# Cross-attention kernel: the running sum of the probabilities built by accumulating transfers in three chains

## The chip, the cores and the metric

The kernel runs on one core of one Trainium2 chip, in a single launch. The metric is the device time in microseconds; lower is better. One core has TensorE (matrix products into the accumulation memory PSUM), VectorE, ScalarE and GpSimd (element-wise work), SyncE (here it issues the loads and stores) and 16 DMA engines that all queues share. In the rows below they are PE (PEld for its weight loads), DVE, ACT, POOL and SP.

## What is computed

One transformer layer on 8 batches of 56 tokens of width 128. Cross-attention with 16 heads of 64 over 1500 context vectors per batch, then a feed-forward block of width 512 with one expert per batch; both on a layer-normalised input and added back.

```python
kv = context @ Wkv;  k, v = jnp.split(kv, 2, axis=-1);  q = x @ Wq
dots = jnp.einsum('bhnd,bhmd->bhnm', q, k) * SCALE
dots = dots - (1.0 - mask)[:, None, :, None] * 1e6
attn = jax.nn.softmax(dots, axis=-1)
out  = jnp.einsum('bhnm,bhmd->bhnd', attn, v)          # then @ Wout + bout
# layer: x = x + attention(layernorm(x), ctx);  x = x + ffn(layernorm(x))
```

The softmax needs, for each of the 56 x 16 = 896 pairs of token and head, the sum of 1500 exponentials. This sum is what the change is about.

## The kernel before

**Folding.** Wq and Wk are multiplied at the start to `w_qk`, Wv and Wout to `w_vo`, so that scores and values are taken against the context itself. `qk` holds the folded queries of all batches, 896 columns per batch. Scores are computed in three products of rounded parts: `ctxt_hi` and `qk_hi` (rounded, cast by VectorE) and `ctxt_lo`, `qk_lo` (what the rounding left, subtracted by GpSimd).

**Tiles.** The 1500 context vectors of a batch are 12 tiles (`TM`) of 125 rows (`MT`). For tile t TensorE writes the scores into PSUM (`scores`, L373), ScalarE takes the exponential into slot t % 6 of the ring `ex` (`exponentials`, L597) and fills PSUM with the shift of tile t + 2 (`seed`, L607), and two tiles later TensorE multiplies the exponentials with the context (`probs_ctx`, L412). VectorE adds tile t - 1 to `ex_sum` at step t (`add_tile`, L755): 11 additions of 125x896 per batch, the last at step 0 of the next batch. At step 3 of the next batch TensorE multiplies `ex_sum` by a matrix of ones (`sum_jobs`, L435), which adds up the 125 rows, ScalarE takes the inverse through a logarithm and an exponential (`inverse_sums`, L620), and VectorE refines it (`drain_sum`, `refine_inverse`).

**Order.** Each engine has an order written out by hand: an `iteration` over t = 0 to 11 per batch, with the places of all smaller work in lists such as `MAX_AT` and `SUM_AT` (L121 to L141). TensorE's smaller products go through `job` (L333), which uses two PSUM banks in turn and waits until VectorE has emptied the one before the last. 21 of them per batch give the maxima of the next batch's scores (`max_job`, L428, emptied by `max_part`, L764). Batches are taken in pairs; in every second iteration the feed-forward block of a pair runs too. Batches 0 and 7 stand outside the loop.

**GpSimd** clears an identity matrix, subtracts the low parts of batch 0, and then, at t = 2, 3, 6 and 7, those of the next batch (`iteration`, L1016). Nothing in it waits for the pace of the tiles. **SyncE** loads a batch's transposed context (`load_ctxt`, L270) once the low parts of the batch before are subtracted, and the plain context (`load_ctx`, L276) once the products of the batch two before are done.

**Who may write over an exponential.** ScalarE writes tile t into its slot after TensorE's product with tile t - 6 and VectorE's addition of it:

```python
wait(act, pv_done, b.at(TM, t - RING + 1))
wait(act, ex_summed, b.at(TM - 1, max(t - RING, 1)) if t >= RING else b.at(TM - 1, t - RING + 1))
```

**At the start** the raw Wq and Wk lie in the memory of `ex`. **At the end**, for batch 7, VectorE adds the last tile, TensorE does the sum job, and the inverse, the output projection and the feed-forward block of the last half pair follow one after another.

Of the kernel before, what the change touches and what calls it, by code (L numbers as in the profile page):

```python
# [32 lines left out]
ALU = mybir.AluOpType  # L33
# [10 lines left out]
P = 128  # L44
# [56 lines left out]
def xattn_ffn(nc, x_pairs, ctx, ctx_t, mask_q, wq_t, wk_t, wv_t, w_out, b_out, w1, b1_t, w2, b2, out):  # L101
# [15 lines left out]
    RING = 6  # L117
    assert D == P and MT * TM == M and QT * P == Q and MC * KM == M and E == B and TM % RING == 0

# [29 lines left out]
    with ExitStack() as stack:  # L149
# [15 lines left out]

        ex = sb("ex", [P, RING, Q])
        ex_sum = sb("ex_sum", [P, 2, Q])
# [9 lines left out]
        wqk_raw = ex[:, :, :].rearrange("p r q -> p (r q)")[:, 0:2 * HP * P].rearrange("p (w j d) -> p w j d", w=2, j=HP)  # L177
# [26 lines left out]
        hid = sb("hid", [P, 2 * FT, TOK])  # L204
        hid_u = sb("hid_u", [P, 2 * FT, TOK])
        hid_e = sb("hid_e", [P, 2 * FT, TOK])
# [34 lines left out]

        block = stack.enter_context(nc.Block())

# [86 lines left out]
        def _(pe):  # L330
# [81 lines left out]
            def probs_ctx(b, t, between=None):  # L412

                u = b.parity
                pe.wait_ge(ex_ready, b.at(TM, t + 1))
                if t == 0:
                    pe.wait_ge(ctx_in[b.parity], b.at_every_other(16, 16))
                    wait(pe, att_ready, b.at(1, 0))
                    if b.i is None and b.off == 0:
                        pe.wait_ge(later_drained, HEADS)  # L420
                for c in range(2):
                    if c == 1 and between is not None:
                        between()
                    mm = nc.tensor.matmul(ps_a[:, c, 0:CH], ctx_sb[0:MT, u, t, :], ex[0:MT, t % RING, c * CH:(c + 1) * CH],  # L424
                                          start=(t == 0), stop=(t == TM - 1))
                mm.then_inc(pv_done, 1)
# [8 lines left out]
            def sum_jobs(b):  # L435

                pe.wait_ge(ex_summed, b.at(TM - 1, TM - 1))
                for c in range(2):
                    nc.tensor.matmul(job()[:, 0:CH], ones[0:MT, :], ex_sum[0:MT, b.parity, c * CH:(c + 1) * CH],  # L439
                                     start=True, stop=True).then_inc(job_ready, 1)  # L440
# [152 lines left out]
        def _(act):  # L593
# [3 lines left out]
            def exponentials(b, t):  # L597

                slot = t % RING
                src = ps_s[0:MT, t % 2, :, 0:CH]  # L600
                act.wait_ge(scores_ready, b.at(TM, t + 1))

                wait(act, pv_done, b.at(TM, t - RING + 1))
                wait(act, ex_summed, b.at(TM - 1, max(t - RING, 1)) if t >= RING else b.at(TM - 1, t - RING + 1))
                nc.scalar.activation(half(ex[0:MT, slot, :]), src, ACT.Exp, scale=SCALE).then_inc(ex_ready, 1)  # L605
# [132 lines left out]
        def _(dve):  # L738
# [16 lines left out]
            def add_tile(b, t):  # L755

                dve.wait_ge(ex_ready, b.at(TM, t + 1))
                dst = ex_sum[0:MT, b.parity, :]
                left = ex[0:MT, 0, :] if t == 1 else dst
                if t > 1:  # L760
                    dve.wait_ge(ex_summed, b.at(TM - 1, t - 1))
                nc.vector.tensor_tensor(dst, left, ex[0:MT, t % RING, :], ALU.add).then_inc(ex_summed, 1)  # L762
# [114 lines left out]
            def iteration(b, prepare=True, pair=None):  # L877
# [40 lines left out]
                for t in range(TM):  # L918
                    drain((t, 0))
                    between((t, 0))  # L920
                    if t > 1:
                        add_tile(b, t - 1)
                    elif t == 0 and b.off > 0:
                        add_tile(b.later(-1), TM - 1)
# [59 lines left out]
            add_tile(last, TM - 1)  # L984
# [15 lines left out]
        def _(pool):  # L1000
# [14 lines left out]

            def iteration(b, prepare=True):  # L1016
                for t in range(TM):
                    if b.off == 0 and t == FOLD_AT[-1][0] + 2:
# [5 lines left out]
                    if prepare and t in CTXT_LO_AT:  # L1024
# [5 lines left out]
                                    pattern=[[-1, P]], channel_multiplier=1).then_inc(ident_ready, 1)  # L1030
            for k in range(KM):
# [68 lines left out]
```

## Time and profile before

| | us |
|---|---|
| median of 3 runs | 408.41 (407.51 to 409.65) |
| profiled execution, its own time | 407.78 |
| its span | 406.0 |
| TensorE busy | 394.8 (97%) |
| TensorE, loading weights (beside its products) | 285.1 (70%) |
| VectorE busy | 302.7 (75%) |
| ScalarE busy | 206.1 (51%) |
| GpSimd busy | 57.6 (14%) |
| share of the 16 DMA engines | 15.5%, 19.45 MB |

The granted clock of TensorE is at full speed in all 40 slices. The span runs from the first to the last instruction; the execution's own time is 1.78 us longer. A busy time is a mean over the span and says nothing by itself of who waits for whom.

### The profile page before, as it was taken

To read this page: it belongs to the slowest core of one execution; us is meant where nothing else is said; L and a number is where in the kernel's file an instruction comes from. 1 tells how busy PE (TensorE), PEld (TensorE's weight loads), DVE (VectorE), ACT (ScalarE), POOL (GpSimd) and SP (SyncE) were. 2 spreads that over 40 slices of the span, in tenths; PEclk is the share of its full clock that TensorE was granted. 3 is DMA by queue.
4 is the path that set the end of the run, shared out by engine and by line. 5 is a ranking of instruction groups with operands and counts; after the bars stand their busy time and mean duration, and the time that the engine had idled before them with its cause. 6 is when DMAs were issued, how large, how long until landed. Compare 5 with 4: busy or idle time off the path is not lost.

```text
span 406.0 us, 5555 instructions
## 1 busy us (share of the span) xinstructions
PE 394.8 (97%) x1721; PEld 285.1 (70%) x1721; DVE 302.7 (75%) x490; ACT 206.1 (51%) x274; POOL 57.6 (14%) x47
## 2 busy tenths in 40 slices
PE   8998999999999999999999999999999999999995
PEld 7765777766776876767676877667776776676684
DVE  4889578878797689877887689877887687365443
ACT  3546354466437445565556444665366444755431
POOL 0603040600060000600060001500060000000000
PEclk9999999999999999999999999999999999999999
DMA  7660020050005000043005000161011001200000
GB/s 252 206 200 19 2 76 1 2 147 5 2 0 141 12 2 2 13 127 120 0 7 144 0 0 0 35 173 53 0 30 45 0 0 39 70 2 0 3 2 3
DMA packets 20661, 19.62 MB, mean 48 GB/s; under 512 B 904, under 2 KB 17576, under 8 KB 20648
## 3 DMA queue, kind: packets, MB, share of 16 engines
q1 hardware_dynamic: 20648, 19.45, 15.5%
q8 instruction: 8, 0.13, 0.1%
q14 instruction: 5, 0.04, 0.0%
HBM read 19.21 MB, written 0.23 MB: 48 GB/s over the span
## 4 chain that ended last, share of the span: by engine, by line
PE 93%; DVE 4%; ACT 2%; issue 1%; ACTq 0%
PE ps_a L424 35%; PE ps_s L396 28%; PE ps_x L432 10%; PE ps_x L451 4%; PE ps_x L439 3%; PE ps_a L371 2%; PE ps_s L526 2%; PE ps_x L471 2%; PE ps_x L480 2%; PE ps_s L410 2%; PE ps_x L344 1%; PE ps_s L364 1%; DVE log_sum L793 1%; PE ps_a L344 1%; ACT inv_sum L635 1%
## 5 line engine op out<-in xcount | busy, mean ns | idle before, releaser
L424 PE MATMUL ps_a<-ex,ctx_sb 125*128 125x448 f32 x384 | 172.2, 541 | 0.0
L605 ACT ACTIVATE ex<-ps_s 125x896 f32<-125x896 f32 x96 | 88.0, 917 | 118.9 <-PE ps_s L396 92.8
L765 DVE TENSOR_REDUCE chunk_max<-ps_x 128x1 f32<-128x500 f32 x168 | 111.2, 673 | 31.9 <-PE ps_x L432 28.9
L432 PE MATMUL ps_x<-ctxt_hi,qk_hi 128*128 128x500 f32 x168 | 88.6, 530 | 4.9 <-DVE log_sum L793 3.6
L424 PEld LDWEIGHTS ps_a<-ex,ctx_sb 125*128 125x128 f32 x384 | 71.3, 189 | 27.6 <-issue 21.6
L762 DVE TENSOR_TENSOR ex_sum<-ex_sum,ex 125x896 f32<-125x896 f32 x80 | 86.5, 1081 | 4.6 <-ACT ex L605 4.6
L396 PE MATMUL ps_s<-qk_hi,ctxt_hi 128*125 128x448 f32 x192 | 87.1, 535 | 0.0
L612 ACT COPY ps_s<-shift_row 125x896 f32<-125x896 f32 x80 | 72.9, 911 | 9.9 <-DVE shift_row L882 7.8
L396 PEld LDWEIGHTS ps_s<-qk_hi,ctxt_hi 128*125 128x125 f32 x192 | 35.8, 187 | 35.5 <-issue 35.1
L396 PE MATMUL ps_s<-qk_hi,ctxt_lo 128*125 128x448 f32 x192 | 57.2, 379 | 0.0
L396 PE MATMUL ps_s<-qk_lo,ctxt_hi 128*125 128x448 f32 x192 | 54.7, 366 | 0.0
L1007 POOL TENSOR_TENSOR qk_lo<-qk,qk_hi 128x448 fp32r<-128x448 f32 x16 | 23.7, 1483 | 217.5 <-DVE qk_hi L786 216.0
L432 PEld LDWEIGHTS ps_x<-ctxt_hi,qk_hi 128*128 128x128 f32 x168 | 31.5, 188 | 24.8 <-issue 8.1
L396 PEld LDWEIGHTS ps_s<-qk_hi,ctxt_lo 128*125 128x125 f32 x192 | 35.6, 186 | 6.8 <-issue 2.6
L396 PEld LDWEIGHTS ps_s<-qk_lo,ctxt_hi 128*125 128x125 f32 x192 | 35.6, 185 | 3.3
L1013 POOL TENSOR_TENSOR ctxt_lo<-ctxt_raw,ctxt_hi 128x500 fp32r<-128x500 f32 x24 | 32.0, 1348 | 11.3 <-DVE ctxt_hi L782 11.3
L782 DVE CAST ctxt_hi<-ctxt_raw 128x500 fp32r<-128x500 f32 x24 | 23.7, 1019 | 0.0
L793 DVE TENSOR_TENSOR log_sum<-ps_x,inv_sum 128x448 f32<-128x448 f32 x16 | 9.3, 619 | 18.6 <-ACT inv_sum L635 18.6
L451 PEld LDWEIGHTS ps_x<-w_vo,att_n 128*128 128x128 f32 (+1 forms) x160 | 18.1, 170 | 1.5 <-issue 1.2
L451 PE MATMUL ps_x<-w_vo,att_n 128*128 128x128 f32 (+1 forms) x160 | 18.6, 275 | 0.0
L629 ACT ACTIVATE log_sum<-ps_x 128x448 f32<-128x448 f32 x16 | 8.7, 542 | 10.7 <-PE ps_x L439 10.6
L648 ACT ACTIVATE logv<-veps 128x1 f32<-128x1 f32 (+2 forms) x7 | 1.4, 203 | 24.7 <-DVE veps L828 22.5
(79 smaller groups left out, 272.4 us busy)
## 6 DMA issues: line engine op xcount, KB each, us to landing
ctxt_raw<-in_ctx_t SPq DMA_DIRECT2D x8, 750.0 KB, 7.3
ctx_sb<-in_ctx SPq DMA_DIRECT2D x8, 750.0 KB
w_sb<-in_w SPq DMA_DIRECT2D x4, 512.0 KB, 3.7
w_sb<-in_w SPq DMA_DIRECT2D x8, 256.0 KB, 4.3
ex<-in_wq_t SPq DMA_DIRECT2D x2, 256.0 KB, 3.8
ex<-in_wk_t SPq DMA_DIRECT2D x2, 256.0 KB, 4.6
att_n<-in_wv_t SPq DMA_DIRECT2D x1, 512.0 KB, 6.0
att_n<-in_w_out SPq DMA_DIRECT2D x1, 512.0 KB, 6.8
```

The costliest lines, as they stand in the source:

```text
L396: mm = nc.tensor.matmul(dst[c], a[:, u, rows], q[:, u, chunks[c]], start=(n == 0 and not seed), stop=(n == 2 and seed), skip_group_check=seed)
L424: mm = nc.tensor.matmul(ps_a[:, c, 0:CH], ctx_sb[0:MT, u, t, :], ex[0:MT, t % RING, c * CH:(c + 1) * CH], start=(t == 0), stop=(t == TM - 1))
L432: nc.tensor.matmul(bank[:, 0:MC], qk_hi[:, u, t * P:(t + 1) * P], ctxt_hi[:, u, k * MC:(k + 1) * MC], start=True, stop=True).then_inc(job_ ...
L451: mm = nc.tensor.matmul(bank[pair.tokens(), 0:D], att_n[:, h, pair.tokens()], w_vo[:, h, :], start=(h == 0), stop=(h == HEADS - 1))
L605: nc.scalar.activation(half(ex[0:MT, slot, :]), src, ACT.Exp, scale=SCALE).then_inc(ex_ready, 1)
L612: nc.scalar.copy(ps_s[0:MT, t % 2, :, 0:CH], half(shift_row[0:MT, :])).then_inc(seeded, 1)
L762: nc.vector.tensor_tensor(dst, left, ex[0:MT, t % RING, :], ALU.add).then_inc(ex_summed, 1)
L765: nc.vector.tensor_reduce(chunk_max[:, k, t:t + 1], filled()[:, 0:MC], AX.X, ALU.max).then_inc(job_free, 1)
L782: nc.vector.tensor_copy(ctxt_hi[:, b.parity, k * MC:(k + 1) * MC], ctxt_raw[:, k * MC:(k + 1) * MC]).then_inc(ctxt_hi_ready, 1)
L793: nc.vector.tensor_tensor(log_sum[:, cols], bank[:, 0:CH], inv_sum[:, cols], ALU.mult).then_inc(job_free, 1)
L1007: nc.gpsimd.tensor_tensor(qk_lo[:, b.parity, cols], b.pick(qk)[:, cols], qk_hi[:, b.parity, cols].bitcast(F32), ALU.subtract).then_inc(qk_ ...
L1013: nc.gpsimd.tensor_tensor(ctxt_lo[:, b.parity, cols], ctxt_raw[:, cols], ctxt_hi[:, b.parity, cols].bitcast(F32), ALU.subtract).then_inc(c ...
```

## The change

Tiles 0, 1 and 2 of a batch are no longer written into the ring but into three accumulators, `ex_first`, which exist twice, for even and odd batches. The ring `ex_ring` has four slots and holds tiles 3 to 11 in turn. GpSimd issues one DMA for each of tiles 3 to 10 that adds the tile, 128 partitions by 896 numbers, to accumulator t % 3 (`add_by_dma`). The three chains are 0, 3, 6, 9; 1, 4, 7, 10; and 2, 5, 8. A transfer waits for the one before it in its chain. VectorE makes three additions per batch (`add_to_sum`), at steps 0, 1 and 2 of the next batch: tile 11 to the third accumulator, then the first and the second accumulator to it. ScalarE's exponential waits for the transfer that reads its slot instead of VectorE's addition. GpSimd clears the part of the accumulators that doesn't hold the raw Wq and Wk, and the ring, at the start, because the transfers take all 128 partitions and the exponentials write 125. The raw weights lie in `ex_first`. The tiles of the feed-forward block (`hid`, `hid_u`, `hid_e`) lie in the memory of `w_qk`, which is no longer read by then.

```diff
@@ -114,8 +114,8 @@
     TOK = 64
-    RING = 6
-    assert D == P and MT * TM == M and QT * P == Q and MC * KM == M and E == B and TM % RING == 0
+    RING, ACCS, LAST_DMA = 4, 3, 10
+    assert D == P and MT * TM == M and QT * P == Q and MC * KM == M and E == B and ACCS < RING < LAST_DMA < TM
@@ -163,8 +163,8 @@
-        ex = sb("ex", [P, RING, Q])
-        ex_sum = sb("ex_sum", [P, 2, Q])
+        ex_first = sb("ex_first", [P, 2, ACCS, Q])
+        ex_ring = sb("ex_ring", [P, RING, Q])
         shift_diag = sb("shift_diag", [P, QT, P], F32R)
@@ -174,7 +174,7 @@
-        wqk_raw = ex[:, :, :].rearrange("p r q -> p (r q)")[:, 0:2 * HP * P].rearrange("p (w j d) -> p w j d", w=2, j=HP)
+        wqk_raw = ex_first[:, :, :, :].rearrange("p u r q -> p (u r q)")[:, 0:2 * HP * P].rearrange("p (w j d) -> p w j d", w=2, j=HP)
         wvo_raw = att_n[:, :, :].rearrange("p (w j) d -> p w j d", w=2)
@@ -201,9 +201,7 @@
         z_t = sb("z_t", [P, P])
-        hid = sb("hid", [P, 2 * FT, TOK])
-        hid_u = sb("hid_u", [P, 2 * FT, TOK])
-        hid_e = sb("hid_e", [P, 2 * FT, TOK])
+        hid, hid_u, hid_e = (w_qk[:, 4 * k:4 * k + 4, :].rearrange("p (g c) (h n) -> p (g c h) n", g=1, n=TOK) for k in range(3))
         out_sb = sb("out_sb", [P, D])
@@ -239,7 +237,20 @@
+        add_may_go = sem("add_may_go")
+        ex_added = [sem("ex_added_first"), sem("ex_added_second"), sem("ex_added_third")]
+        ADDS = [sum(t % ACCS == j for t in range(ACCS, LAST_DMA + 1)) for j in range(ACCS)]
+        DVE_SUMS = TM - 1 - LAST_DMA + ACCS - 1
+
         block = stack.enter_context(nc.Block())
+
+        def ex(b, t):
+
+            return ex_first[:, b.parity, t, :] if t < ACCS else ex_ring[:, (t - ACCS) % RING, :]
+
+        def dma_added(eng, b, t):
+
+            eng.wait_ge(ex_added[t % ACCS], b.at(16 * ADDS[t % ACCS], 16 * (t // ACCS)))
@@ -421,7 +432,7 @@
                         between()
-                    mm = nc.tensor.matmul(ps_a[:, c, 0:CH], ctx_sb[0:MT, u, t, :], ex[0:MT, t % RING, c * CH:(c + 1) * CH],
+                    mm = nc.tensor.matmul(ps_a[:, c, 0:CH], ctx_sb[0:MT, u, t, :], ex(b, t)[0:MT, c * CH:(c + 1) * CH],
                                           start=(t == 0), stop=(t == TM - 1))
@@ -434,9 +445,9 @@
-                pe.wait_ge(ex_summed, b.at(TM - 1, TM - 1))
+                pe.wait_ge(ex_summed, b.at(DVE_SUMS, DVE_SUMS))
                 for c in range(2):
-                    nc.tensor.matmul(job()[:, 0:CH], ones[0:MT, :], ex_sum[0:MT, b.parity, c * CH:(c + 1) * CH],
+                    nc.tensor.matmul(job()[:, 0:CH], ones[0:MT, :], ex_first[0:MT, b.parity, ACCS - 1, c * CH:(c + 1) * CH],
                                      start=True, stop=True).then_inc(job_ready, 1)
@@ -596,13 +607,21 @@
-                slot = t % RING
                 src = ps_s[0:MT, t % 2, :, 0:CH]
...
-                wait(act, pv_done, b.at(TM, t - RING + 1))
-                wait(act, ex_summed, b.at(TM - 1, max(t - RING, 1)) if t >= RING else b.at(TM - 1, t - RING + 1))
-                nc.scalar.activation(half(ex[0:MT, slot, :]), src, ACT.Exp, scale=SCALE).then_inc(ex_ready, 1)
+                if t >= ACCS + RING:
+                    act.wait_ge(pv_done, b.at(TM, t - RING + 1))
+                    dma_added(act, b, t - RING)
+                elif t >= ACCS and (b.i is not None or b.off > 0):
+                    act.wait_ge(pv_done, b.at(TM, 0))
+                    before = b.later(-1)
+                    last = max(s for s in range(ACCS, TM) if (s - t) % RING == 0)
+                    if last <= LAST_DMA:
+                        dma_added(act, before, last)
+                    else:
+                        act.wait_ge(ex_summed, before.at(DVE_SUMS, last - LAST_DMA))
+                nc.scalar.activation(half(ex(b, t)[0:MT, :]), src, ACT.Exp, scale=SCALE).then_inc(ex_ready, 1)
@@ -752,14 +771,21 @@
-            def add_tile(b, t):
-
-                dve.wait_ge(ex_ready, b.at(TM, t + 1))
-                dst = ex_sum[0:MT, b.parity, :]
-                left = ex[0:MT, 0, :] if t == 1 else dst
-                if t > 1:
-                    dve.wait_ge(ex_summed, b.at(TM - 1, t - 1))
-                nc.vector.tensor_tensor(dst, left, ex[0:MT, t % RING, :], ALU.add).then_inc(ex_summed, 1)
+            def add_to_sum(b, n):
+
+                dst = ex_first[0:MT, b.parity, ACCS - 1, :]
+                if n < TM - 1 - LAST_DMA:
+                    t = LAST_DMA + 1 + n
+                    dve.wait_ge(ex_ready, b.at(TM, t + 1))
+                    dve.wait_ge(pv_done, b.at(TM, ACCS))
+                    dma_added(dve, b, max(s for s in range(LAST_DMA + 1) if s % ACCS == ACCS - 1))
+                    part = ex(b, t)[0:MT, :]
+                else:
+                    j = n - (TM - 1 - LAST_DMA)
+                    dma_added(dve, b, max(s for s in range(LAST_DMA + 1) if s % ACCS == j))
+                    part = ex_first[0:MT, b.parity, j, :]
+                wait(dve, ex_summed, b.at(DVE_SUMS, n))
+                nc.vector.tensor_tensor(dst, dst, part, ALU.add).then_inc(ex_summed, 1)
@@ -918,10 +944,8 @@
                     between((t, 0))
-                    if t > 1:
-                        add_tile(b, t - 1)
-                    elif t == 0 and b.off > 0:
-                        add_tile(b.later(-1), TM - 1)
+                    if t < DVE_SUMS and b.off > 0:
+                        add_to_sum(b.later(-1), t)
                     between((t, 1))
@@ -981,7 +1005,8 @@
             iteration(last, prepare=False, pair=Pair(None, ROUNDS, half=0))
-            add_tile(last, TM - 1)
+            for n in range(DVE_SUMS):
+                add_to_sum(last, n)
             for c in range(2):
@@ -1013,8 +1038,20 @@
+            def add_by_dma(b, t):
+
+                pool.wait_ge(ex_ready, b.at(TM, t + 1))
+                if t < 2 * ACCS:
+                    pool.wait_ge(pv_done, b.at(TM, t % ACCS + 1))
+                else:
+                    dma_added(pool, b, t - ACCS)
+                pool.sem_inc(add_may_go, 1)
+                pool.dma_start(ex_first[:, b.parity, t % ACCS, :], ex(b, t), accum_op=ALU.add).then_inc(ex_added[t % ACCS], 16)
+
             def iteration(b, prepare=True):
                 for t in range(TM):
+                    if ACCS < t <= LAST_DMA + 1:
+                        add_by_dma(b, t - 1)
                     if b.off == 0 and t == FOLD_AT[-1][0] + 2:
@@ -1028,6 +1065,8 @@
                                     pattern=[[-1, P]], channel_multiplier=1).then_inc(ident_ready, 1)
+            nc.gpsimd.memset(ex_first[:, :, :, :].rearrange("p u r q -> p (u r q)")[:, 2 * HP * P:], 0.0)
+            nc.gpsimd.memset(ex_ring[:, :, :], 0.0)
             for k in range(KM):
```

## Rows read from the trace of the kernel before

**Rows 1.** The page's busy times: engine, busy us (share of span), instructions.

```profile
PE 394.8 (97%) x1721; PEld 285.1 (70%) x1721; DVE 302.7 (75%) x490; ACT 206.1 (51%) x274; POOL 57.6 (14%) x47
```

**Rows 2.** Chain that ended last, in order of time: start us, us, what.

```profile
84.46 1.52 PE ps_x L439 x4
...
125.55 1.52 PE ps_x L439 x4
...
173.86 1.52 PE ps_x L439 x4
```

**Rows 3.** Waits of TensorE: who for whom, us in total, times, longest.

```profile
PE ps_x L432 <- DVE log_sum L793: 3.6, 6, 0.6
...
PE ps_x L432 <- DVE chunk_max L765: 1.0, 1, 1.0
```

**Rows 4.** Page, costliest groups: out<-in forms xcount, busy us, mean ns, idle before.

```profile
L762 DVE TENSOR_TENSOR ex_sum<-ex_sum,ex 125x896 f32<-125x896 f32 x80 | 86.5, 1081 | 4.6 <-ACT ex L605 4.6
```

**Rows 5.** Timeline, batch 2's iteration: start us, us, engine, line, what.

```profile
119.81 1.48 DVE L765 TENSOR_REDUCE chunk_max<-ps_x 128x1 f32<-128x500 f32 x2
...
121.98 0.38 PE L432 MATMUL ps_x<-ctxt_hi,qk_hi 128*128 128x500 f32 x1
```

**Rows 6.** Timeline, exponentials of tiles 3, 7 and 10 of batch 1.

```profile
87.38 0.91 ACT L605 ACTIVATE ex<-ps_s 125x896 f32<-125x896 f32 x1
...
100.00 0.92 ACT L605 ACTIVATE ex<-ps_s 125x896 f32<-125x896 f32 x1 [1.25 <-PE ps_s L396]
...
109.62 0.92 ACT L605 ACTIVATE ex<-ps_s 125x896 f32<-125x896 f32 x1 [1.32 <-PE ps_s L396]
```

**Rows 7.** Timeline, VectorE, batch 2's iteration: first cast, addition at t = 2.

```profile
115.62 1.36 DVE L782 CAST ctxt_hi<-ctxt_raw 128x500 fp32r<-128x500 f32 x1
...
123.00 1.08 DVE L762 TENSOR_TENSOR ex_sum<-ex 125x896 f32<-125x896 f32 x1
```

**Rows 8.** DMA issues: queue, count, KB each, median us to landing.

```profile
ctxt_raw<-in_ctx_t SPq DMA_DIRECT2D x8, 750.0 KB, 7.3
...
w_sb<-in_w SPq DMA_DIRECT2D x4, 512.0 KB, 3.7
...
x_tok<-in_x SPq DMA_DIRECT2D x1, 256.0 KB, 2.7
```

**Rows 9.** Timeline of SyncE: time that issuing a DMA took.

```profile
1.22 0.42 SPq L268 DMA_DIRECT2D ex<-in_wq_t  x1
...
81.19 5.03 SPq L274 DMA_DIRECT2D ctxt_raw<-in_ctx_t  x1
```

**Rows 10.** Groups of GpSimd: its subtraction and its clearing of 2048 elements.

```profile
L1013 POOL TENSOR_TENSOR ctxt_lo<-ctxt_raw,ctxt_hi 128x500 fp32r<-128x500 f32 x24 | 32.0, 1348 | 11.3 <-DVE ctxt_hi L782 11.3
...
L1021 POOL MEMSET att_n<- 128x2048 f32 x1 | 1.8, 1805 | 13.9 <-DVE chunk_max L765 13.9
```

**Rows 11.** Windows, a stretch of loads: busy by engine, clock, DMA share, GB/s.

```profile
181.00:190.00 9.00, 9.00 (x36) 6.56 (x35) 7.17 (x11) 5.12 (x6) 0.00 (x0) 1.00 0.57 196
```

**Rows 12.** Timeline of the start: GpSimd's instructions, VectorE's normalisation and copy.

```profile
1.19 0.29 POOL L1029 TENSOR_SCALAR_AFFINE_SELECT ident<-ident 128x128 f32<-128x128 f32 x1 [0.24 <-POOL ident L1027]
...
5.96 0.34 DVE L945 TENSOR_SCALAR log_sum<-x_tok,meanvar,rstd 128x128 f32<-128x128 f32 x1
...
7.84 0.29 DVE L874 COPY inv_sum<-ps_x 128x128 f32<-128x128 f32 x1 [1.53 <-PE ps_x L519]
...
10.60 4.09 POOL L1013 TENSOR_TENSOR ctxt_lo<-ctxt_raw,ctxt_hi 128x500 fp32r<-128x500 f32 x3 [9.12 <-DVE ctxt_hi L782]
```

**Rows 13.** Timeline, VectorE, the same cast with GpSimd quiet.

```profile
32.02 0.41 DVE L782 CAST ctxt_hi<-ctxt_raw 128x500 fp32r<-128x500 f32 x1
```

**Rows 14.** Timeline of the end: exponential of tile 10, last addition, sum job.

```profile
377.75 0.92 ACT L605 ACTIVATE ex<-ps_s 125x896 f32<-125x896 f32 x1 [0.52 <-PE ps_s L396]
...
382.45 1.07 DVE L762 TENSOR_TENSOR ex_sum<-ex_sum,ex 125x896 f32<-125x896 f32 x1
...
386.00 1.67 PE L439 MATMUL ps_x<-ex_sum,ones 125*128 125x448 f32 x4
```

## The prediction, made before the changed kernel had run

> **What bounds the kernel now.** I read the busy times first: TensorE works 394.8 us of a span of 406.0 us, VectorE 302.7, ScalarE 206.1, GpSimd 57.6 [rows 1]. The reader should see that the engine which the change unloads is not the one that is full. The chain that ended last, in order of time, gives the pace: its sum jobs stand at 84.46, 125.55 and 173.86, so an iteration lasts 41.1 us, or 48.3 where a pair's output runs too [rows 2]. Then the waits of TensorE: inside the loop it waits for VectorE six times, 3.6 us in all, for the multiplication that empties the column sums, and once for a maximum, 1.0 us [rows 3]. The 3.6 us stay whatever VectorE's load, because that multiplication itself waits for ScalarE's exponential of the logarithm. So the body runs at the pace of TensorE's columns, and an edit gains there only by taking columns off TensorE. This one takes none.
>
> **What leaves VectorE.** Eleven additions of 125x896 per batch, 88 in all, at 1081 ns [rows 4] become three per batch, 24 in all. 88 x 1.08 = 95.1 us falls to 25.9 us, so VectorE's busy time falls by 69 us, to about 234. Of that, TensorE sees at most the 1.0 us wait for a maximum: the other work of VectorE fits already. I take 0 (bounds: a gain of 1.0 us, or 4.6 us if the 3.6 us went too).
>
> **The step at t = 1.** Before, VectorE had no addition at t = 1; now it joins the first chain there, 1.08 us between the last cast and the first two maxima. In batch 2 those two run from 119.81 to 121.29, and TensorE's third maximum job, which needs the first one's bank, starts at 121.98 [rows 5]. Moved back by 1.08, the first maximum (half of 1.48 us) ends at about 121.6 and the second at 122.3, in front of the jobs that need their banks (the fourth, 0.63 us after the third, about 122.6). Slack 0.3 us, cost 0; if it misses, up to 1.08 us in each of seven iterations, 7.6 us. At t = 0 an addition stood before, and so did one at t = 2.
>
> **The eight transfers per batch.** Nothing in this trace accumulates by DMA or is issued from GpSimd, so three costs are unknown: GpSimd's issue, the time to landing, and how much of the 16 DMA engines one takes. What covers them is read from the times of the exponentials. In batch 1 tile 3's ends at 87.38 + 0.91 = 88.3, tile 7's starts at 100.0, tile 10's ends at 109.62 + 0.92 = 110.5 [rows 6]; that is 3.2 us per tile. Three deadlines follow. (a) Exponential t writes over tile t-4 of the ring of four, so each transfer of tiles 3 to 7 has 100.0 - 88.3 = 11.7 us to land. Behind that wait stand ScalarE's seed and the next scores, so a miss reaches TensorE within a tile. (b) VectorE needs the last transfer, tile 10's, at t = 2 of the next iteration, where the addition started at 123.00 [rows 7]: 12.5 us after its exponential. Behind that addition stands the sum job of TensorE, at 125.55 in the chain [rows 2], 2.5 us later. (c) All eight must be served between 88.3 and 123.0: 34.7 us.
>
> Time to landing: plain loads took 2.7 us for 256 KB, 3.7 for 512 KB and 7.3 for 750 KB [rows 8]. One transfer here is 128 x 896 x 4 bytes = 448 KB. Interpolated, a plain one lands in 3.45 us. An accumulating one must also read its destination; I add the slope once more, 448 x 1.0/256 = 1.75, which gives 5.2 us. Lower bound 3.45, upper bound twice the 7.3 us row by its bytes, 2 x 7.3 x 448/750 = 8.7 us. GpSimd's issue: a DMA issue on the other queue took 0.42 us, and 5.03 us where that queue was full [rows 9]; GpSimd's own subtraction takes 1.35 [rows 10]. I take 1.3. Together 6.5 us (3.9 to 13.7), inside (a) and (b) at the value taken. GpSimd pays 64 x 1.3 = 83 us and was idle for 348.
>
> Share of the DMA engines: at 181 to 190 us loads moved 196 GB/s with the engines 57% busy, 344 GB/s when full [rows 11]. By that a plain 448 KB takes 1.3 us of all engines, a doubled one 2.7. The load of the next transposed context takes 2.2 us more of the same window at that rate. Eight times 2.7 + 2.2 + 2 for the last landing = 26 us against 34.7. The limit is (34.7 - 4.2)/8 = 3.8 us each. I take 2.7, cost 0; both ends are 1.3 and 8.7. A collective's reduce step is put down to its second source read and not to the adder in the Trainium skill, Collectives: The Full Stack, section The bandwidth ceiling; doubling once more is that rule, and no row here can show it.
>
> **What moves on GpSimd and SyncE.** The three subtractions for the next batch's low halves stood at t = 2, 6 and 7 only in program order: GpSimd ran ahead of them. Now transfers stand between, each waiting for its exponential, so the last subtraction comes behind tile 6's transfer, whose exponential starts 3.2 us before tile 7's and ends at 97.7 [rows 6]. Add 1.3 and 1.35: 100.4. SyncE issues the next load of the transposed context after it, where it did so at 81.19 [rows 9]. VectorE's first cast needs it at 115.62 [rows 7]: 15 us for a transfer of 7.3. Cost 0; at twice the time, 14.6 us, still 0. TensorE needs the low halves only at the next t = 0. ScalarE's exponential has one more wait, which costs nothing while (a) holds.
>
> **The start.** GpSimd clears 6912 elements per partition. It cleared 2048 in 1.8 us [rows 10], so 6.1 us, from 1.5 (its last instruction, 1.19 + 0.29) to 7.6, before its first subtraction at 10.60 [rows 12]. Hidden by 3 us, cost 0. If VectorE's copies can't run beside it, the normalisation due at 5.96 ends at 7.9 instead of 6.3, and the copy at 7.84, which needs a transposition between them, starts some 0.5 us late [rows 12]. That such a thing exists is seen in the cast of 128x500: 0.41 us with GpSimd quiet, 1.36 us beside its subtraction [rows 13]. Bounds 0 and 1.1 us (two such blocks), value 0. The Trainium skill, SBUF — State Buffer, Who interferes with whom, says that VectorE's two-port copies and GpSimd lock each other out for a whole instruction; by it the start would be 0.5 us later and the sum 0.5 us higher. The cast rows agree for subtractions; no row shows a clear beside a copy.
>
> **The end.** This is the one place without cover. Before, the last addition ran at 382.45 and was done at 383.5, while TensorE's products went on until the sum job at 386.00 [rows 14]. Now three additions stand there in a row: tile 11 at 382.45 to 383.5, first chain to 384.6, second chain (tile 10 in it) to 385.7 if its transfer has landed by 384.6. Tile 10's exponential ends at 377.75 + 0.92 = 378.7 [rows 14]; plus 6.5 it lands at 385.2. The last addition is then done at 386.3, the hand-over takes 0.15, and the sum job starts at 386.45: 0.5 us later. Nothing runs beside it from there. Lower end 0 (landing by 384.6), upper end with 13.7: landing 392.4, sum job 393.6, 7.6 us. With the upper landing alone (8.7 + 1.3): 388.7, sum job 389.9, 3.9 us.
>
> **Sum.** The profiled execution took 407.78 us, 1.78 more than its span. 407.78 + 0 (body) + 0 (start) + 0.5 (end) = 408.3. The median of the runs before lies 0.63 above the profiled execution, so the forecast is 408.9 us.
>
> **Rivals.**
> 1. The body is hidden, but a transfer lands later than I take: 10 to 13.7 us after its exponential. For it: every row of a transfer is of another kind and another queue. Against: 512 KB in 3.7 us. End 3.9 to 7.6 us later, body at the edge of deadline (a). Time: 408.4 + 3.9 = 412.3, up to 416.
> 2. The other side: the DMA engines (or GpSimd's issue) can't serve one accumulation per tile. It decides above 3.8 us each. At 4.36 (the 7.3 us row by bytes, once) the eight need 8 x 4.36 + 4.2 = 39.1 us against 34.7: 4.4 us per batch. The long iterations have 7 us more room than the short ones [rows 2]. Four short ones give 18 us: 426. At 5.03 (the blocked issue) 8 x 5.03 + 4.2 - 34.7 = 9.7, in the short ones 39 us and 3 x 2.7 = 8 in the long: 455. At 8.7 the transfers alone are 64 x 8.7 = 557 us: above 600. For it: an addition in the path of a DMA is nowhere in this trace. Against: the rate rows leave 1.1 us per transfer even with the second read.
> 3. VectorE's relief gives back what TensorE waits for it in the body: 4.6 us, 408.4 - 4.6 = 403.8. Against: 3.6 of them wait for ScalarE.
> That the transfers aren't made, or that VectorE keeps its additions, I exclude by the diff.
>
> **How the numbers follow.** Forecast (hidden body, end 0 to 1.6 us, start 0 to 1.1 us; own range 407.6 to 410.4) 0.60. Rival 1: 0.12. Rival 2: 0.22. Rival 3: 0.06. About 0.5%, 2.0 us, is what a measurement of this kernel can tell from no change. Faster by more is rival 3: 0.06. Same is the forecast and the near edge of rival 1: 0.62. Slower is the rest: 0.32. The range runs from 407.0 (below the forecast's lower edge; rival 3 left out, 0.06) to 428, which takes in rival 1 and the mild case of rival 2 and leaves out about 0.14.
>
> **What would show it.** VectorE's busy time near 234 us with 24 additions of 125x896. TensorE's waits in the body still the 3.6 us after the sums and no wait of ScalarE for a transfer. Landing times near 5 us and a share of the DMA engines up from 15% by some 64 x 2.7/406 = 43 points. In the last batch, the third addition ending near 386.3 and the sum job right behind it. I am wrong if TensorE's busy share falls in the short iterations with ScalarE or VectorE waiting for a DMA ahead of it (rival 2), if the gap at the end is over 2 us (rival 1), or if iterations get shorter than 41 us (rival 3).

## The result, and the profile after

The changed kernel takes 414.4 us (median of 4 runs, 413.8 to 417.6) against 408.3 before: 1.017 times as long (1.014 to 1.019). That is inside the range I gave, and on the side that I gave 0.32. The likeliest case, no change, did not happen. The profiled execution took 414.44 us with a span of 412.6, 6.6 more than before.

The page of the changed kernel: busy times, the new DMA queue, the issues on GpSimd, and the time to landing. They answer to [rows 1, 8].

```profile
PE 397.5 (96%) x1721; PEld 286.5 (69%) x1721; DVE 255.1 (62%) x426; ACT 206.1 (50%) x274; POOL 117.8 (29%) x113
...
q0 software_dynamic: 9216, 29.36, 38.4%
...
L1049 POOL DMA_DIRECT2D ex_first<-ex_ring x64 | 55.9, 873 | 224.7 <-ACT ex_ring L624 221.2
...
ex_first<-ex_ring POOLq DMA_DIRECT2D x64, 448.0 KB, 4.4
```

VectorE fell from 302.7 to 255.1 us, not to 234. Some 13 us of the 21 are instructions that became longer: without the two collisions found below (experiment 3) VectorE is busy 241.8 us. Where the other 8 are was not tested; a record of an addition overlaps the next one's by up to 0.1 us (133.05 + 1.08 against 134.05 in experiment 9), so that leaving 64 out frees less than 64 x 1.08. TensorE, whose work is the same, rose by 2.7: some of it ran at a lower clock. The 64 transfers took 0.87 us each to issue, 4.4 us to land and 38.4% of the DMA engines, 2.5 us each.

Where the 6.6 us are is seen by comparing the starts of the 96 exponentials in the two traces. The lag is 4.67 us at the very first and stays there within 0.2 us through batches 0 and 1. It grows by some 0.6 us in each of batches 2, 4 and 6, most of it between tiles 7 and 9 (taken at tile 2 of batches 1, 3, 5 and 7 it is 4.67, 5.30, 5.95 and 6.55), and is 6.56 at the last one and at the last sum job. So there are two places, and the end is not one of them.

**The start.** Timeline of the changed kernel (start us, us, engine, line, what); the last row is the first exponential:

```profile
1.43 2.87 POOL L1068 MEMSET ex_first<- 128x3328 f32 x1
...
1.52 5.88 DVE L977 TENSOR_SCALAR ident<-ident 128x128 f32<-128x128 f32 x1 [0.25 <-POOL ident L1066]
...
4.24 3.09 POOL L1069 MEMSET ex_ring<- 128x3584 f32 x1
...
9.63 0.34 DVE L969 TENSOR_SCALAR log_sum<-x_tok,meanvar,rstd 128x128 f32<-128x128 f32 x1
...
10.60 0.29 DVE L900 COPY inv_sum<-ps_x 128x128 f32<-128x128 f32 x1 [0.63 <-PE ps_x L530]
...
10.94 3.76 PE L375 MATMUL ps_s<-inv_sum,w_qk 128*128 128x112 f32 x16 [0.38 <-DVE inv_sum L900]
...
37.01 0.92 ACT L624 ACTIVATE ex_first<-ps_s 125x896 f32<-125x896 f32 x1 [0.45 <-PE ps_s L421]
```

VectorE's first multiplication, 0.23 us of work, took 5.88 us: it ended 0.07 us after GpSimd's second clear did. The normalisation that stood at 5.96 us [rows 12] came at 9.63 and the copy at 10.60 instead of 7.84. The same two rows of before, the query products and the first exponential:

```profile
8.31 2.01 PE L364 MATMUL ps_s<-inv_sum,w_qk 128*128 128x112 f32 x16 [0.51 <-ACT w_qk L689]
...
32.34 0.92 ACT L605 ACTIVATE ex<-ps_s 125x896 f32<-125x896 f32 x1 [0.46 <-PE ps_s L410]
```

The query products begin 2.6 us later and then take 3.76 us instead of 2.01. Windows from 10 to 14 and from 14 to 16 us (length, busy us and instructions of PE, PEld, DVE, ACT and POOL, granted clock, DMA share, GB/s) of the changed kernel, then the first of them for the kernel before:

```profile
10.00:14.00 4.00, 3.50 (x15) 3.24 (x16) 2.70 (x11) 0.78 (x2) 1.14 (x1) 0.50 0.76 288
...
14.00:16.00 2.00, 2.00 (x12) 1.67 (x12) 0.62 (x2) 0.78 (x2) 2.00 (x3) 0.62 0.36 109
```

```profile
10.00:14.00 4.00, 4.00 (x25) 2.86 (x24) 3.17 (x8) 2.19 (x5) 3.40 (x3) 1.00 0.75 290
```

TensorE had idled, and ran this stretch at half of full speed, 1.2 instead of 2.4 GHz: the granted clock fell at 8.7 us, during a wait from 8.1 to 10.1, and was back at 15.5. The two add up: 2.63 of delay and 1.75 in the query products are 4.4 of the 4.67.

**The pair iterations.** Sum jobs in the chain, to be read beside [rows 2]: the short iteration still takes 41.1 us, the long one 48.9 instead of 48.3.

```profile
89.13 1.52 PE ps_x L450 x4
...
130.21 1.52 PE ps_x L450 x4
...
179.16 1.52 PE ps_x L450 x4
```

Timeline of the changed kernel at tile 6 of batch 2, and the same normalisation before:

```profile
147.69 0.87 POOL L1049 DMA_DIRECT2D ex_first<-ex_ring  x1 [4.54 <-ACT ex_ring L624]
...
147.70 2.25 DVE L859 TENSOR_SCALAR z<-x,meanvar,rstd 128x128 f32<-128x128 f32 x1
...
148.29 1.56 POOL L1038 TENSOR_TENSOR ctxt_lo<-ctxt_raw,ctxt_hi 128x500 fp32r<-128x500 f32 x1
...
150.66 0.33 PE L472 MATMUL ps_x<-ident,z 128*128 128x128 f32 x1 [0.42 <-DVE chunk_max L791]
```

```profile
144.02 0.34 DVE L833 TENSOR_SCALAR z<-x,meanvar,rstd 128x128 f32<-128x128 f32 x1
```

The normalisation `z` took 2.25 us instead of 0.34. It ended with GpSimd's subtraction, which used to run at step 1 and now stands behind tile 6's transfer. VectorE's maxima come late behind it, and TensorE waits for a bank before it can transpose `z`.

TensorE's waits, to be read beside [rows 3]. The second and the last are the start (there TensorE waits for the normalised input and, before that, for raw weights), the third the three pair iterations, with 1.2 of the 1.9 us that these lose; the other two are as before.

```profile
PE ps_x L443 <- DVE log_sum L819: 3.6, 6, 0.6
...
PE ps_x L530 <- DVE log_sum L969: 2.0, 1, 2.0
...
PE ps_x L472 <- DVE chunk_max L791: 1.2, 3, 0.4
...
PE ps_x L443 <- DVE chunk_max L791: 1.0, 1, 1.0
...
PE ps_a L355 <- DMA ex_first<-in_wk_t: 0.8, 1, 0.8
```

**The end.** To be read beside [rows 14]: exponential of tile 10, its transfer's issue, the three additions, the sum job.

```profile
384.31 0.92 ACT L624 ACTIVATE ex_ring<-ps_s 125x896 f32<-125x896 f32 x1 [0.52 <-PE ps_s L407]
...
385.83 0.86 POOL L1049 DMA_DIRECT2D ex_first<-ex_ring  x1 [1.86 <-ACT ex_ring L624]
...
389.01 1.07 DVE L788 TENSOR_TENSOR ex_first<-ex_first,ex_ring 125x896 f32<-125x896 f32 x1
...
390.19 2.29 DVE L788 TENSOR_TENSOR ex_first<-ex_first 125x896 f32<-125x896 f32 x2
...
392.56 1.74 PE L450 MATMUL ps_x<-ex_first,ones 125*128 125x448 f32 x4
```

Products and additions finish together: the sum job is as far behind the exponential as before, 8.25 us in both.

### The profile page after: what moved, and what is told of

Read it like the earlier page. It is cut to its first block, busy times and chain, and to the rows that moved or that the text cites. A ratio compares the mean times of both kernels' runs of the same rounds, so it can differ in the third digit from the quotient of the medians.

```text
span 412.6 us, 5552 instructions
## 1 busy us (share of the span) xinstructions
PE 397.5 (96%) x1721; PEld 286.5 (69%) x1721; DVE 255.1 (62%) x426; ACT 206.1 (50%) x274; POOL 117.8 (29%) x113
## 3 DMA queue, kind: packets, MB, share of 16 engines
q0 software_dynamic: 9216, 29.36, 38.4%
## 4 chain that ended last, share of the span: by engine, by line
PE 88%; DVE 7%; issue 3%; ACT 1%; POOL 0%; DVEq 0%; ACTq 0%; POOLq 0%
PE ps_a L435 33%; PE ps_s L407 26%; PE ps_x L443 10%; PE ps_x L462 4%; PE ps_x L450 3%; PE ps_a L382 2%; PE ps_x L482 2%; PE ps_x L491 2%; PE ps_s L421 2%; DVE ident L977 1%; PE ps_s L375 1%; PE ps_x L355 1%; DVE chunk_max L791 1%; DVE log_sum L819 1%; ACT inv_sum L654 1%
## 5 line engine op out<-in xcount | busy, mean ns | idle before, releaser
L435 PE MATMUL ps_a<-ex_ring,ctx_sb 125*128 125x448 f32 x288 | 128.8, 541 | 0.0
L1049 POOL DMA_DIRECT2D ex_first<-ex_ring x64 | 55.9, 873 | 224.7 <-ACT ex_ring L624 221.2
L624 ACT ACTIVATE ex_ring<-ps_s 125x896 f32<-125x896 f32 x72 | 66.0, 917 | 92.8 <-PE ps_s L407 91.5
L435 PEld LDWEIGHTS ps_a<-ex_ring,ctx_sb 125*128 125x128 f32 x288 | 53.4, 190 | 21.2 <-issue 17.0
L435 PE MATMUL ps_a<-ex_first,ctx_sb 125*128 125x448 f32 x96 | 43.6, 540 | 0.0
L1038 POOL TENSOR_TENSOR ctxt_lo<-ctxt_raw,ctxt_hi 128x500 fp32r<-128x500 f32 x24 | 35.1, 1465 | 8.7 <-DVE ctxt_hi L808 8.7
L624 ACT ACTIVATE ex_first<-ps_s 125x896 f32<-125x896 f32 x24 | 22.1, 919 | 29.1 <-PE ps_s L421 27.8
L808 DVE CAST ctxt_hi<-ctxt_raw 128x500 fp32r<-128x500 f32 x24 | 22.8, 980 | 0.0
L435 PEld LDWEIGHTS ps_a<-ex_first,ctx_sb 125*128 125x128 f32 x96 | 18.0, 189 | 5.7 <-issue 4.0
```

The source lines that it names most:

```text
L624: nc.scalar.activation(half(ex(b, t)[0:MT, :]), src, ACT.Exp, scale=SCALE).then_inc(ex_ready, 1)
L808: nc.vector.tensor_copy(ctxt_hi[:, b.parity, k * MC:(k + 1) * MC], ctxt_raw[:, k * MC:(k + 1) * MC]).then_inc(ctxt_hi_ready, 1)
L1038: nc.gpsimd.tensor_tensor(ctxt_lo[:, b.parity, cols], ctxt_raw[:, cols], ctxt_hi[:, b.parity, cols].bitcast(F32), ALU.subtract).then_inc(c ...
L1049: pool.dma_start(ex_first[:, b.parity, t % ACCS, :], ex(b, t), accum_op=ALU.add).then_inc(ex_added[t % ACCS], 16)
```

## The experiments

Each ran beside the kernel before on the same chip, whose medians were 408.0 to 408.2. The first exponential's start varies by up to 1 us between profiled executions that do the same there (31.95 to 32.90 in the five versions with the clears moved behind), so smaller differences between two profiles are not read there; inside one profile the lag is steadier.

### 1. The clears moved behind (e1)

```diff
-memset(ex_first rest); memset(ex_ring)      # ahead of batch 0's subtractions
+qk_lo_chunk(0, 0); memset(ex_first rest); memset(ex_ring); qk_lo_chunk(0, 1)
```

> The changed kernel with GpSimd's two clears moved from the front to between its two subtractions of the first queries' low half (about 17 to 23 us), where VectorE does only maxima and additions. Theory A (VectorE's constant multiplication at 1.5 us is locked out by the clears, 5.88 us instead of 0.23, and TensorE's first work slips 2.6 us and then runs at half clock, 4.67 us in all): that multiplication back to 0.23 us, no stretch at half clock, first exponential near 32.3 instead of 37.0, time 414.3 - 4.7 = 409.7. Rival S (the start is late because the raw weights now land elsewhere and TensorE waits 0.8 us for them): no change, 414.3.

Measured 410.3, ratio 1.0054 (1.0034 to 1.0073). The first exponential starts at 32.9. Its timeline, VectorE's first multiplication and the `z` of batch 2:

```profile
1.52 0.23 DVE L977 TENSOR_SCALAR ident<-ident 128x128 f32<-128x128 f32 x1 [0.24 <-POOL ident L1066]
...
143.64 2.25 DVE L859 TENSOR_SCALAR z<-x,meanvar,rstd 128x128 f32<-128x128 f32 x1
```

4.1 of the 6.1 us are gone and the first operation is short again; `z` is as long as in the changed kernel. Rival S is out: the raw weights lie where the changed kernel has them. A wait for them can come even so without harm: in e12, which has these clears too, it is 0.9 us, and the first exponential starts at 32.34, as in the kernel before.

### 2. The subtractions moved ahead (e2)

```diff
-CTXT_LO_AT, QK_LO_AT = [2, 6, 7], [2, 3]
+CTXT_LO_AT, QK_LO_AT = [1, 2, 3], [2, 3]
```

> The changed kernel with the three subtractions of the context's low parts at t = 1, 2, 3 of GpSimd's order instead of 2, 6, 7, so that they run ahead of the transfers as they did before. Theory B (in the pair iterations the normalisation at t = 6 takes 2.25 us instead of 0.34 because GpSimd's second subtraction runs beside it, 0.63 us each, 1.9 us in three): normalisation at most 1.2 us (the issue of the transfer, 0.87 us, may still lock it), the three steps of 0.63 us gone, time 414.3 - 1.9 = 412.4. Rival T (it is the issue of the transfer alone that locks VectorE): normalisation still near 1.2 us, and part of the 1.9 stays: 413.3. Rival U (traffic of the transfers slows VectorE): normalisation stays at 2.2, time 414.3.

Measured 411.9, 2.5 less than the changed kernel. Timeline, `z` of batch 2 and the transfer's issue beside it:

```profile
150.28 0.86 POOL L1049 DMA_DIRECT2D ex_first<-ex_ring  x1 [5.81 <-ACT ex_ring L624]
...
150.30 0.35 DVE L859 TENSOR_SCALAR z<-x,meanvar,rstd 128x128 f32<-128x128 f32 x1
```

With the issue beside it and the subtraction away, `z` takes 0.35 us, and no wait for a maximum before the transposition is left. So it is the subtraction (theory B), not the issue (rival T) and not the traffic (rival U). The edit gave 0.6 us more than B said; experiment 3 shows that 0.9 us come from the iteration of batch 0.

### 3. Both (e3)

```diff
+qk_lo_chunk(0, 0); memset(ex_first rest); memset(ex_ring); qk_lo_chunk(0, 1)
+CTXT_LO_AT, QK_LO_AT = [1, 2, 3], [2, 3]
```

> Both edits: clears behind, subtractions ahead. Theories A and B together: 414.3 - 4.7 - 1.9 = 407.7, that is the kernel before within 0.5 us, since nothing else of the change is on the path. If the transfers or the two joining additions cost anything of their own, it is what remains above 408.3.

Measured 407.2, ratio 0.9975 (0.9961 to 0.9989): a little faster than before. 0.9 us of it lie in the iteration of batch 0. Timelines there, first of this version, then of the kernel before: GpSimd's first subtraction beside the casts, the casts, and TensorE's maximum job with its wait.

```profile
32.31 1.26 POOL L1038 TENSOR_TENSOR ctxt_lo<-ctxt_raw,ctxt_hi 128x500 fp32r<-128x500 f32 x1 [9.80 <-DVE ctxt_hi L808]
...
33.41 1.74 DVE L808 CAST ctxt_hi<-ctxt_raw 128x500 fp32r<-128x500 f32 x2
...
35.78 0.49 PE L443 MATMUL ps_x<-ctxt_hi,qk_hi 128*128 128x500 f32 x1 [0.15 <-DVE chunk_max L791]
```

```profile
33.41 1.25 POOL L1013 TENSOR_TENSOR ctxt_lo<-ctxt_raw,ctxt_hi 128x500 fp32r<-128x500 f32 x1
...
33.61 2.62 DVE L782 CAST ctxt_hi<-ctxt_raw 128x500 fp32r<-128x500 f32 x2
...
36.87 0.50 PE L432 MATMUL ps_x<-ctxt_hi,qk_hi 128*128 128x500 f32 x1 [1.03 <-DVE chunk_max L765]
```

With another order on GpSimd the two casts take 1.74 us instead of 2.62, and the wait of 1.03 us [rows 3] shrinks to 0.15. The same drop of the lag, 0.9 us at tile 2 of batch 0, stands in the traces of e2 and e9.

### 4. The kernel before with the clears alone (e4)

```diff
+nc.gpsimd.memset(ex rest, 3328 columns); nc.gpsimd.memset(spare, 3584 columns)   # at the front
```

> The kernel before with nothing added but the two clears by GpSimd at its front (3328 elements of the ring, 3584 of a spare tile); no transfers, additions as before. Theory A: VectorE's multiplication takes about 5.9 us, first exponential near 37.0, time 408.3 + 4.7 = 413.0. Rival S, or any that needs the transfers: 408.3.

Measured 412.3, ratio 1.0112 (1.0074 to 1.0151); single runs up to 416.1. VectorE's first multiplication, and the window from 14 to 20 us:

```profile
1.51 5.88 DVE L954 TENSOR_SCALAR ident<-ident 128x128 f32<-128x128 f32 x1 [0.24 <-POOL ident L1030]
```

```profile
14.00:20.00 6.00, 6.00 (x25) 4.79 (x23) 2.30 (x3) 1.36 (x3) 4.03 (x4) 0.50 0.64 162
```

The half clock's end, window from 22 to 24 us:

```profile
22.00:24.00 2.00, 2.00 (x13) 1.92 (x12) 0.72 (x2) 0.78 (x2) 0.00 (x0) 0.63 1.01 355
```

No transfer is needed for the loss at the start. The median is 4.1 us above the kernel before. In the profiled execution (415.9 us) the granted clock fell at 9.8 us and was back only at 23.4, with TensorE busy all the time from 11 us on, and the first exponential came 8.0 us late; in experiment 2's profile it is 8.1. In the changed kernel's profile the half clock lasted 6.8 us. So behind the same clears the half clock lasts 7 us in some executions and 14 in others. What decides is not shown: TensorE's waits differ too (2.4 and 2.3 us in the two long cases; 0.8 for the raw weights and then 2.0 in the short one). Experiment 4's six runs fall into two groups, 411.9 to 412.7 and 415.9 to 416.1, with a mean granted clock of 0.992 to 0.996 and 0.982. The changed kernel's run of 417.6 us, at 0.983 against 0.990 to 0.994, looks like the long case; it has no trace.

### 5. The wait filled with idle products (e5)

An idle product is one whose result nobody uses.

```diff
 pe.wait_ge(ident_ready, 1)
+keep_clock(12)
 xnt_job(0, 1, 1)
```

> The changed kernel as it is (clears at the front), with twelve idle products of 128 columns on TensorE ahead of the first transposition, where it waits 2.0 us for the normalised input. Theory A splits the 4.67 us of the start into 2.6 us of waiting and some 2 us of half clock behind it (the 16 query products take 3.76 us instead of 2.01). With the wait filled, the granted clock stays at full speed in the stretch from 10 to 14 us and the time falls by about 2 us: 412.3. Rival K (the half clock doesn't come from the wait, or the clock was low anyway): the stretch stays at 0.5 and the time at 414.3.

Measured 412.8 (412.3 to 414.6), 1.6 less than the changed kernel. Window from 10 to 14 us:

```profile
10.00:14.00 4.00, 3.62 (x30) 3.24 (x29) 3.46 (x13) 1.56 (x4) 1.34 (x1) 1.00 0.78 294
```

The clock stayed full and the first exponential came 2.3 us late: the delay is left, the half clock gone. Rival K is out.

### 6. No transfers (e6)

```diff
-pool.dma_start(ex_first[...], ex(b, t), accum_op=ALU.add).then_inc(ex_added[t % ACCS], 16)
+pool.sem_inc(ex_added[t % ACCS], 16)
```

> The version with both edits (clears behind, subtractions ahead), its 64 transfers left out; GpSimd raises their semaphores itself when it would issue them, so tiles 3 to 10 are missing from the sums. What the transfers cost anywhere shows as the difference to the version with both edits, 407.2. Theory C (they are hidden throughout): 407.2 within 0.3 us. Rival E (the end: tile 10's landing sets the last sum job): up to 0.5 us less, 406.7, with the sum job earlier relative to the products before it. Rival D (issue or traffic slows other engines in the body): more than 1 us less.

Measured 407.3, against 407.2 with all 64 transfers (its sums are incomplete, as said). From the last exponential to the sum job it is 5.52 us in both. The transfers and their issue cost nothing on the path (theory C).

### 7. GpSimd's order alone, in the kernel before (e9)

```diff
-CTXT_LO_AT, QK_LO_AT = [2, 6, 7], [2, 3]
+CTXT_LO_AT, QK_LO_AT = [1, 2, 3], [2, 3]
```

> The kernel before with one edit: GpSimd subtracts the first low part of the context ahead of that of the queries (steps 1, 2, 3 instead of 2, 6, 7). In the version with both edits the first iteration lost 0.9 us less than in the kernel before, where TensorE waits 1.03 us for a maximum because two casts took 2.62 us beside GpSimd. Theory F (that gain is GpSimd's order, not the change): the same here, 408.2 - 0.9 = 407.3, equal to the version with both edits. Rival V (it is VectorE's relief): 408.2, and the change with both edits keeps a gain of 1 us of its own.

Measured 407.2, ratio 0.9967 (0.9948 to 0.9987). The whole gain of experiment 3 is the order of GpSimd. Up to here the transfers are worth nothing.

### 8. One maximum job moved (e7, e12)

```diff
-(2, 2), (3, 2), (4, 0), (4, 2), (5, 0), (5, 2), (6, 0),
+(2, 2), (4, 0), (4, 2), (5, 0), (5, 1), (5, 2), (6, 0),
```

> The version with both edits, and the maximum job at (3, 2), the first after the column sums, moved to (5, 1) in both lists. Theory G (TensorE's six waits of 0.6 us there, 3.6 us, come from asking for a bank before ScalarE's inverse and VectorE's multiplication have emptied it; one step later it is free): the waits vanish, time 407.2 - 3.6 = 403.6. Rival H (the bank is just as late for the next job, at (4, 0)): unchanged, 407.2. Rival J (three maxima at t = 5 overload VectorE's two banks there): some of it comes back as waits for maxima, 405 to 407.

> The version with both edits and the moved maximum once more, for comparison on the same chip: 402.4.

Measured 402.4, ratio 0.985 (0.982 to 0.989), and 402.6, 0.989 (0.986 to 0.991). The waits for `log_sum` are gone, and no wait for maxima has come in their place: theory G, not H or J. The gain is 4.8 and 4.5 us, 4.7 in the mean, 1.1 more than the waits listed: each iteration became 0.8 us shorter, not 0.6. Where the other 0.2 come from is not shown.

### 9. The same move without transfers (e10, e13)

> The kernel before with GpSimd's order as in the last run of it and the maximum job at (3, 2) moved to (5, 1); no transfers, VectorE keeps its eleven additions per batch. The same move took 4.8 us from the version with transfers (407.2 to 402.4). Theory W (the move frees TensorE's wait for the column sums and has nothing to do with VectorE's load): the same here, 402.4, and the transfers are worth nothing. Rival X (VectorE, 75% busy, can't empty three banks at t = 5 with an addition between them; with 60% it can): part of the gain is lost to waits for maxima, 403.5 to 406, and that part is what the transfers are worth.

Measured 407.0: no gain against experiment 7. By the starts of the exponentials each short iteration became 0.7 us shorter and each pair iteration 0.7 longer. Timelines of the pair iteration, without transfers (e10) and then with them (e12): the addition at step 5, the maxima, TensorE's output projection.

```profile
133.05 1.08 DVE L762 TENSOR_TENSOR ex_sum<-ex_sum,ex 125x896 f32<-125x896 f32 x1
...
134.05 1.25 DVE L765 TENSOR_REDUCE chunk_max<-ps_x 128x1 f32<-128x500 f32 x2
...
134.78 3.84 PE L451 MATMUL ps_x<-w_vo,att_n 128*128 128x128 f32 x32 [1.09 <-DVE chunk_max L765]
```

```profile
131.50 1.31 DVE L791 TENSOR_REDUCE chunk_max<-ps_x 128x1 f32<-128x500 f32 x2
...
132.91 3.79 PE L462 MATMUL ps_x<-w_vo,att_n 128*128 128x128 f32 x32
```

Without transfers VectorE still has an addition between the maxima. It empties the bank late, and TensorE waits 1.09 us for it, three times. With them the projection starts at once. Rival X holds at this place. The last run asks whether another place helps:

```diff
 # batches of even number, against experiment 7: (3, 2) goes to (7, 1); the others to (5, 1)
-(2, 2), (3, 2), (4, 0), ... (7, 0), (8, 0),
+(2, 2), (4, 0), ... (7, 0), (7, 1), (8, 0),
```

> The kernel before with GpSimd's order and the same maximum moved, but in the pair iterations to (7, 1), where VectorE has 0.8 us idle, instead of (5, 1), where in the last run of this kind TensorE waited 1.1 us three times for a maximum; in the others it stays at (5, 1). Question: is the gain of the move out of reach for the kernel without transfers, or was only the place bad? If the place (theory W again): the three waits go, 407.0 - 3 x 1.7 = 402, equal to the version with transfers. If VectorE is too full wherever the maximum goes (rival X): part of it comes back as other waits in the pair iterations, 404 to 407.

Measured 404.0 (403.7 to 404.3), ratio 0.989 (0.986 to 0.992). Most of the gain is to be had without transfers too. TensorE's wait for maxima:

```profile
PE ps_x L432 <- DVE chunk_max L765: 1.5, 5, 0.8
```

What is left to the transfers is 404.0 - 402.5 = 1.5 us, as much as these waits, as far as these two places go; other places, and (7, 1) with transfers, were not tried. The two ran on different chips, each beside the kernel before (408.0 both times).

### 10. The clears behind the first multiplication (e11)

```diff
+pool.wait_ge(scaled, 1)     # set by VectorE's constant multiplication
 memset(ex_first rest); memset(ex_ring)
```

> The changed kernel with the clears still at the front, but waiting until VectorE's constant multiplication (0.23 us at 1.5 us) is done. The lock hits whichever comes second. Theory Y (every one-source operation of VectorE from memory to memory is shut out, the small ones of the normalisation too): the first of these, one number per partition at about 4.0 us, now waits for the clears to end at about 7.7, and nothing is gained: 414. Rival Z (only operations of many columns are shut out; the 128-column normalisation at about 6 us is the first): it ends at about 8.0 instead of 6.3, the copy behind it starts at 8.4 instead of 7.84, most of the 4.7 us is gained: 410.3.

Measured 412.7 (410.9 to 416.8), ratio 1.014 (1.010 to 1.018). Timeline:

```profile
1.81 2.87 POOL L1070 MEMSET ex_first<- 128x3328 f32 x1 [0.32 <-DVE ident L978]
...
4.08 0.15 DVE L965 TENSOR_SCALAR veps<-meanvar 128x1 f32<-128x1 f32 x1
...
4.62 3.09 POOL L1071 MEMSET ex_ring<- 128x3584 f32 x1
...
5.20 2.53 DVE L965 TENSOR_SCALAR veps<-meanvar 128x3 f32<-128x3 f32 x1
...
5.28 2.45 DVE L842 TENSOR_TENSOR corr<-veps,rstd 128x1 f32<-128x1 f32 x1
```

Neither theory. The operation on one number per partition ran in 0.15 us in the middle of a clear. The one on three numbers waited 2.5 us, until the second clear ended at 7.71, and with it the operation queued behind. The first exponential came 2.7 us late. So it isn't every operation from memory to memory that is shut out; whether the number of elements decides, these two cases suggest and don't show.

## Why the prediction was right or wrong

- **"TensorE sees at most the 1.0 us wait for a maximum."** Right for this change: 64 additions fewer moved nothing. That 1.0 us wait hung on GpSimd's order and not on VectorE's additions: in e9, which keeps them all, it is gone. The 3.6 us I called fixed "whatever VectorE's load" were fixed only in this order; experiment 8 removed them by asking for the bank later.
- **The step at t = 1, cost 0.** Right: the short iterations kept their 41.1 us.
- **Landing 5.2 + 1.3 us, 2.7 us of the DMA engines each, cost 0.** Right, and a little pessimistic: 4.4 us from the issue and 2.5. The longest landing in the changed kernel took 8.2 us, in experiment 3 it was 10.0 from the issue, close to the 11.7 from the exponential that deadline (a) leaves, and without cost. Rivals 1 and 2 fell. One exponential waited 1.3 us for a transfer, in one batch, without effect on TensorE.
- **The end, 0.5 us.** Too high: 0. I had the transfer landing at 6.5 us after its exponential; with the median of 4.4 us it landed at about 390.2 (an estimate from 385.83 + 4.4), ahead of the third addition at 391.4. The additions follow each other, and they end at 392.48, just as the products do.
- **"Hidden by 3 us, cost 0", the start.** This is the step that failed. The clears lasted 6.0 us, as worked out, and ended in time for GpSimd's own work; but they shut VectorE out. I had named this and bounded it at 1.1 us, since I looked only at the normalisation at 5.96 and the copy at 7.84 (and put the copy 0.5 us late; with the 0.63 us that the changed kernel shows between the two it would be 0.7). The multiplication at 1.5 us stood first in VectorE's queue and held everything behind it for 5.9 us, and I left out what a late start does to TensorE's clock. It cost 4.7 us in the profiled execution, and 4.1 by the medians of experiments 1 and 4; experiment 5 shows that the clock is 1.6 of it.
- **"Cost 0", the moved subtractions.** Failed as well. I followed who waits for the subtraction (the next load, 15 us of room, right) and not what runs beside it at its new place. It cost 1.9 us by the lags; experiment 2 gives 2.5, with the 0.9 of batch 0 in it.
- **Rival 3, VectorE's relief.** Wrong for the change as made.

The forecast was no change, and the kernel became slower by 6.1 us. That the range held is luck: its upper part stood there for late landings and full DMA engines, and neither happened. The rule of the Trainium skill (SBUF — State Buffer, Who interferes with whom), that two-port copies of VectorE and GpSimd's instructions shut each other out for a whole instruction, was the one to follow through the whole queue. The 5.88 us agree with it, and the multiplication stayed out across two clears in a row. The 2.25 us agree only in part: the same rule lets the one that issues first go first, and by the trace that was VectorE.

## What to carry to other kernels

Unloading an engine that wasn't full brought nothing by itself here. What lost or gained time was the order of the small jobs around it: one maximum job moved was worth 4.7 us with the relief, and 0 or 3.2 without it, by its place. When work is put on GpSimd, list what VectorE does from memory to memory during it, from the first instruction on, and take the head of VectorE's queue as late by the whole length of GpSimd's work. An instruction that is hidden by its own waiters can still be a neighbour that costs.

## What the runs showed of the hardware

- Accumulating transfers of 448 KB from GpSimd, memory to memory on the chip: 0.87 us to issue, 4.4 us to landing (4.2 to 8.2; up to 10.0 in experiment 3), 2.5 us of all 16 engines, no measurable cost beside a TensorE that is 97% busy (407.2 with, 407.3 without them).
- Issuing one did not lengthen a VectorE normalisation of 128x128 beside it (0.35 us), while a subtraction of 128x500 on GpSimd did (2.25 us). In that case VectorE had started 0.6 us before the subtraction. Why it didn't finish first is not shown; GpSimd's spans are rough.
- Beside a clear on GpSimd, VectorE's operation on one number per partition took 0.15 us and that on three numbers 2.53 us.
- After a wait of 2.0 to 2.4 us at the start TensorE was granted half clock, 1.2 GHz, for 6.8 us in one profile (8.7 to 15.5 us) and for some 14 us in two others (9.8 to 23.4 and 10.1 to 23.7), though it was busy nearly all the time from 11 us on; with the wait filled it stayed at 2.4 GHz.
